# Attention and mixture-of-experts kernel: projection pieces in other quarters of a step, q and k first in a unit

## What is computed

```python
q = (x @ Wq.T + bq).reshape(b, s, 16, 16)             # layer 1; k and v alike
attn = softmax(einsum('bqhd,bkhd->bhqk', q, k) / 4)
x = layernorm(x + (einsum('bhqk,bkhd->bqhd', attn * head_mask, v).reshape(b, s, 256) @ Wo.T + bo))
n = rmsnorm(x, g1)                                    # layer 2
q = q * cos + rotate_half(q) * sin                    # of n @ wq; k alike
h = x + softmax(causal(q @ k.T / 4)) @ v @ wo
logits = rmsnorm(h, g2) @ w_router
y = h + sum over the best 2 experts of weight * (silu(n @ wg) * (n @ wu)) @ wd
x = layernorm(x + y)
```

## Time and profile before

| | us |
|---|---|
| median of 3 runs | 1440.64 (1439.84 to 1443.2) |
| profiled execution | 1439.77 |
| its span, first to last instruction | 1438.0 |
| TensorE busy | 1271.7 (88%) |
| VectorE busy | 956.0 (66%) |
| ScalarE busy | 827.7 (58%) |
| GpSimd busy | 797.1 (55%) |
| mean share of TensorE's clock granted | 0.948 |

### The profile page before, as it was taken

One profiled execution on the slowest core, in us unless ns is written; L12 is line 12 of the kernel. 1 busy time (PEld: TensorE's weight loads), 2 busy tenths in 40 slices (PEclk: granted clock), 3 DMA queues, 4 the chain that ended last, 5 costly groups with the idle time before them and its releaser, 6 DMA issues. The chain is left out here.

```text
span 1438.0 us, 33091 instructions
## 1 busy us (share of the span) xinstructions
PE 1271.7 (88%) x11455; PEld 705.8 (49%) x11456; DVE 956.0 (66%) x1760; ACT 827.7 (58%) x1673; POOL 797.1 (55%) x835
## 2 busy tenths in 40 slices
PE   4999999999989999899999963399999999999990
PEld 1222322223223443344444432378888888888880
DVE  7888888988897888887898613734444444444443
ACT  4178788888878767566667741134434433444334
POOL 5144557547456665856554234056666666666644
PEclk9799999999999999999999975599999999999995
DMA  6345767767687787868675434693322222322326
GB/s 186 69 97 166 174 181 205 202 192 201 180 212 202 224 234 205 228 203 220 175 178 165 120 99 145 182 275 52 46 43 44 47 46 43 47 43 44 44 31 241
DMA packets 159005, 204.46 MB, mean 142 GB/s; under 512 B 31217, under 2 KB 121329, under 8 KB 158897
## 3 DMA queue, kind: packets, MB, share of 16 engines
q1 hardware_dynamic: 141424, 182.55, 46.3%
q0 software_dynamic: 17472, 20.50, 9.1%
HBM read 111.46 MB, written 82.87 MB: 135 GB/s over the span
## 5 line engine op out<-in xcount | busy, mean ns | idle before, releaser
L978 ACT ACTIVATE a_probs<-a_ps_s 128x512 f32<-128x512 f32 (+2 forms) x896 | 459.9, 569 | 156.1 <-PE a_ps_s L746 150.9
L1053 DVE TENSOR_REDUCE a_shift_max<-a_ps_m 128x1 f16<-128x512 f32 x512 | 320.4, 682 | 50.1 <-PE a_ps_m L751 48.8
L751 PE MATMUL a_ps_m<-a_qkx 48*128 48x128 f16 (+3 forms) x1408 | 284.1, 301 | 19.7 <-DVE a_shift_max L1053 9.7
L1650 PE MATMUL e_ps_gu<-e_xT,w_up 128*128 128x256 f16 x2574 | 297.2, 274 | 2.6 <-ACT e_xT L1704 2.6
L746 PE MATMUL a_ps_s<-a_qkx 49*128 49x128 f16 (+3 forms) x1408 | 276.1, 296 | 15.1 <-ACT a_probs L978 15.1
L1650 PEld LDWEIGHTS e_ps_gu<-e_xT,w_up 128*128 x2574 | 249.4, 98 | 35.5 <-issue 6.5
L847 PE MATMUL a_ps_o<-a_probs,a_v_one 128*32 128x512 f32 (+3 forms) x2048 | 234.2, 530 | 2.7 <-ACT a_o L985 2.6
L746 PEld LDWEIGHTS a_ps_s<-a_qkx 49*128 49x128 f16 x1408 | 90.0, 95 | 267.3 <-ACT a_probs L978 155.7
L1586 POOL DMA_INDIRECT h<-e_y,e_put x78 | 125.1, 1604 | 88.8 <-DVE e_y L1746 57.6
L448 POOL TENSOR_TENSOR a_o_half<-a_o_half,a_inv_half 128x512 f32<-128x512 f32 x32 | 40.6, 1269 | 227.3 <-DMA a_inv_half<-a_inv_dram 221.9
L1672 PE MATMUL e_ps_y<-w_down,e_h 128*128 x1326 | 154.1, 273 | 9.3 <-issue 6.7
(11 more groups left out here) (194 smaller groups left out, 1664.4 us busy)
## 6 DMA issues: line engine op xcount, KB each, us to landing
a_qkx<-a_qk_dram SPq DMA_DIRECT2D x192, 128.0 KB, 4.3
a_qk_dram<-a_qk SPq DMA_DIRECT2D x32, 512.0 KB
a_o_dram<-a_o SPq DMA_DIRECT2D x64, 256.0 KB, 2.6
a_o_half<-a_o_dram SPq DMA_DIRECT2D x32, 256.0 KB
a_inv_half<-a_inv_dram SPq DMA_DIRECT2D x32, 256.0 KB
part<-a_part SPq DMA_DIRECT2D x16, 512.0 KB, 5.8
a_q_swap<-a_q SPq DMA_DIRECT2D x64, 128.0 KB
spare<-in_wg SPq DMA_DIRECT2D x16, 352.0 KB, 5.6
```

Of the source, the lines that this page charges most:

```text
L751: return pe.matmul(out, qx[first:first + 48, r, pair, q * P:(q + 1) * P], kx[first:first + 48, r, pair, k0:k1], start=start, stop=stop)
L978: act.activation(dst, src, ACT.Exp).then_inc(exp_out, 1)
L1053: vector.tensor_reduce(out, src, AX.X, ALU.max, negate=True).then_inc(max_out, 1)
L1650: mm = pe.matmul(ps_gu[:, bank, kind, f % 2], w[:, ds(e, 1)].rearrange("p o f -> p (o f)"), xT[:, s, xh, k, :], start=n == 0, stop=n == 5)
```

## The change

The table of pieces is new, and so is where a piece stands. Heavy pieces have table columns 2 and 3 and are done in quarter 2 of their step and quarter 0 of the next; light ones have columns 0 and 1 and come at the end of the quarters 0 and 2, behind the value product. Quarters 1 and 3 have no piece. q and k of unit u + 2 now are the first heavy pieces of a unit, then v, and the output projection comes in g = 3 instead of g = 2. The chain of a causal half is: pieces up to the first quarter of step 2h - 7; swap, `turn_half` and `rope_cos` in the odd step 2h - 7; `rope_sum`, the splits and the store in the even step 2h - 6; the load in 2h - 5; first use in 2h - 3 as before. x of a causal unit is loaded and transposed two steps sooner.

```diff
         kind, v, k = {
-            (0, 0): ("turn", u + 2, 0), (0, 1): ("turn", u + 2, 1), (0, 2): ("v", u + 1, 0), (0, 3): ("v", u + 1, 1),
-            (1, 0): ("parts", u - 3, 1), (1, 1): ("rows", u, 1), (1, 2): ("qk", u + 2, 0), (1, 3): ("qk", u + 2, 1),
-            (2, 0): ("logits", u - 3, 0), (2, 2): ("out", u - 1, 0), (2, 3): ("out", u - 1, 1),
-            (3, 0): ("parts", u - 2, 0), (3, 1): ("rows", u + 1, 0), (3, 2): ("qk", u + 2, 2),
-            (3, 3): ("qk", u + 2, 3)}.get((g, i), (None, 0, 0))
+            (0, 0): ("parts", u - 3, 0), (0, 2): ("qk", u + 2, 0), (0, 3): ("qk", u + 2, 1),
+            (1, 0): ("rows", u, 1), (1, 1): ("parts", u - 3, 1), (1, 2): ("v", u + 1, 1), (1, 3): ("qk", u + 2, 2),
+            (2, 0): ("logits", u - 3, 0), (2, 1): ("turn", u + 3, 0), (2, 2): ("qk", u + 2, 3), (2, 3): ("out", u - 1, 0),
+            (3, 0): ("rows", u + 1, 0), (3, 1): ("turn", u + 3, 1), (3, 2): ("out", u - 1, 1),
+            (3, 3): ("v", u + 2, 0)}.get((g, i), (None, 0, 0))
...
                 if n % 2 == 0:
-                    swap((n + 6) // 2)
-                    load_qk((n + 4) // 2)
                     if g == 0:
                         store_part(u - 3)
                         load_res(u - 1)
-                    elif u + 3 > 0:
-                        load_x(u + 3)
+                        if u + 3 > 0:
+                            load_x(u + 3)
                     store_o(n - 1)
                     for m in weights_at(n - 1):
                         store_weights(m)
                         load_weights(m + 2)
+                    store_qk((n + 6) // 2)
                     load_o(n // 2 - 1)
                 else:
+                    swap((n + 7) // 2)
+                    load_qk((n + 5) // 2)
                     load_rows((n + 1) // 2)
...
-                    store_qk((n + 5) // 2)
...
                 if n % 2 == 0:
-                    h = (n + 6) // 2
-                    if plain(h // 2):
-                        split_high(h)
-                        split_low(h)
                     if g == 0:
                         factors(u - 2)
-                        split_x(u + 2)
                     else:
                         part_low(u - 2)
-                    turn_half(h)
+                    split_high((n + 6) // 2)
+                    split_low((n + 6) // 2)
+                    if g == 2:
+                        split_x(u + 3)
+                    for m in weights_at(n):
+                        split_weights(m)
                 else:
-                    h = (n + 5) // 2
-                    if causal(h // 2):
-                        split_high(h)
-                        split_low(h)
+                    turn_half((n + 7) // 2)
                     if g == 1:
                         bias(u - 1)
+                    for m in weights_at(n):
+                        split_weights(m)
                     normalise((n - 3) // 2)
                     if g == 3:
                         add_residual(u - 1)
-                for m in weights_at(n):
-                    split_weights(m)
...
+            def heavy_piece(n, quarter):
+
+                piece = piece_at(n - 1, 3) if quarter == 0 else piece_at(n, 2) if quarter == 2 else None
...
+            def light_piece(n, quarter):
+
+                piece = None if quarter % 2 else piece_at(n, quarter // 2)
...
-                    a_piece(n, quarter)
+                    heavy_piece(n, quarter)
...
                         weigh(n, quarter - 2)
+                    light_piece(n, quarter)
...
-                    early = (1 if quarter < 2 else 0) if causal(u) else 3
+                    early = 0 if causal(u) and quarter >= 2 else 1
+                    empty_light(n, quarter)
...
-                elif g == 2 and quarter >= 2:
-                    residual(u - 1, quarter - 2)
...
+                if n % G == 3 and quarter % 2 == 0:
+                    residual(n // G - 1, quarter // 2)
...
                     if n % 2 == 0:
                         if quarter < 2:
-                            rope_cos((n + 6) // 2, quarter)
+                            rope_sum((n + 6) // 2, quarter)
                         elif quarter == 3:
                             join_maxima((n + 2) // 2)
                     else:
-                        if quarter < 2:
-                            rope_sum((n + 5) // 2, quarter)
                         if quarter == 1:
                             invert((n - 3) // 2)
+                        if quarter in (1, 2):
+                            rope_cos((n + 7) // 2, quarter - 1)
```

More of the change, by code:

```diff
@@ L110, in attention_layers @@
     for n in range(FIRST, LAST):
-        for i in range(4):
+        for i in (0, 2, 1, 3):
             if piece_at(n, i):
@@ L714, in a_piece @@
                     turn_maxima(u, k)
-                elif kind == "out":
-                    project_out(u, k)
                 elif kind == "parts":
@@ L932, in move_parts, with empty_piece @@
                 act.activation(nT[:, 0].rearrange("p k s -> p (k s)"), ps_x16[:], ACT.Copy).then_inc(piece_out, 1)
-            def empty_piece(n, i):
-                piece = piece_at(n, i)
+            def empty_piece(n, quarter):
+                piece = piece_at(n, 2) if quarter == 2 else piece_at(n - 1, 3) if quarter == 0 else None
                 if piece is None:
@@ L942, in empty_piece, with empty_light @@
                     move_v(u, k)
-                elif kind == "rows":
+            def empty_light(n, quarter):
+                piece = piece_at(n, quarter // 2) if quarter % 2 else None
+                if piece is None:
+                    return
+                kind, u, k = piece
+                if kind == "rows":
                     move_rows(u, k)
@@ L1232, in _ @@
                 for quarter in range(4):
-                    early = causal((n + 3) // G)
+                    empty_light(n, quarter)
                     for i in range(4):
```

113 lines of the change are left out of this document (63 added, 50 removed).

## The result

| | us |
|---|---|
| kernel before, median of 4 runs on the same chip | 1441.9 (1439.8 to 1448.5) |
| changed kernel, median of 4 runs | 1542.4 (1539.5 to 1554.1) |
| ratio | 1.070, 95% interval 1.064 to 1.077 |
| its profiled execution, and span | 1539.5, 1537.7 |

What follows compares the result with a forecast made beforehand. TensorE, busy 88% of the span, was taken as the bound, with VectorE pacing light quarters. Terms -4.5 - 5.2 - 2.4 - 2.5 - 1.5 + 3.5 = -12.6 us took 1439.8 to 1427.2, median 1428; range 1413 to 1443.

Steps and rivals of the forecast that it cites:

- the one on new waits: SP's queue: load_rows waits no longer than before; load_o behind store_qk hardly later, 0, at most +8 us.
- the sign that the text itself named: Sign of being wrong in the profile after: SP waiting in store_qk with load_o behind it; no size given.
- The quarters, plain half: Plain units 1 to 7: alternating heavy and light quarters save 0.6 to 0.7 us a unit, -4.5 us in all.
- the cover: Plain half: light VectorE load in g = 0 hides 1.2 us more from g = 3; +8 bound if gone.
- the walk: One whole plain unit followed quarter by quarter, each instruction starting when engine, input and bank are there; gave 0.65 us gain.
- VectorE in g = 3: Rival, plain half: the cover in g = 0 fails, +13 us, so 1441; chance 0.10.
- Residual and part_low: Causal half: residual two quarters later no longer waits for GpSimd's part_low; -3.7 us of waits, -5.2 with low clock.
- aT: Transposed attention output from GpSimd: two quarters of delay remove TensorE's four waits, -2.4 us, bound 0.
- The rotary chain: Moving rotary work and splits between odd and even steps halves TensorE's 4.9 us waits for maxima, -2.5 us.
- the rival of the ports: Odd steps feeding or running the causal half: GpSimd holds more VectorE products, +24 us, so 1452; chance 0.10.
- The clock: TensorE's half-clock stretch at 790.3 partly goes once stalled maxima go, -1.5 us, bounds -3.4 and +3.4.
- The start: Unit 0: ScalarE's weight copies start 7.2 us later, delaying low parts and row maxima, +3.5 us, bounds 0 and +7.2.

Runs made afterwards that it cites:

- 1500.3: Changed kernel with load_rows moved ahead of swap and load_qk in SP's odd step; 1500.3 us, ratio 1.042.
- 1482.7: Changed kernel with load_rows first in SP's odd step and load_o ahead of store_qk in the even one; 1482.7 us, ratio 1.029.
- 1456.9: Changed kernel with only load_qk moved to the end of SP's odd step, load_o still behind store_qk; 1456.9 us, ratio 1.009.
- the kernel with both edits: Changed kernel with load_qk last in SP's odd step and load_o ahead of store_qk in the even one; 1444.8 us, ratio 1.003.
- the kernel of 1443.1: The kernel with both edits, but load_qk right behind load_inv, ahead of the weights' stores and loads; 1443.1 us, ratio 1.001.
- the two mended ones: The kernel with both edits and the kernel of 1443.1, both with SP's order changed against the changed kernel; 1444.8 and 1443.1 us.

## Why the prediction was wrong

**The step that failed** is the one on new waits: "so load_rows waits no longer than before", which gives the rows no term at all, and for the denominators 0, "hardly later". It asked whether SP's *instruction* would wait for a semaphore. For the rows that was answered rightly: from 480 to 850 SP waits 1.2 us in all in the swap's, the load's and their own line. For the denominators it was not: SP waits 44.1 us in `store_qk` ahead of `load_o` (3.8 before), the sign that the text itself named. It didn't ask at all what was in the queue ahead of the transfer. Moving swap and load from even to odd steps put ten transfers, 1280 KB, ahead of 8 KB that the next step's first score needs; `store_qk` ahead of `load_o` delays the denominators both ways. The price of SP's order is 98 us, of which 85 are the load's line; `load_o` in its old place was worth 18 us in one pair of kernels (1500.3 and 1482.7) and 12 in another (1456.9 and 1444.8), where the text had 0 with 8 as the bound. The text even listed "swap (four DMAs) and load (six) from even to odd steps", and costed only the slack of the load. In the trace of before denominators, rows and inverse go out ahead of the large transfers; that order was there to be read. The bounds fail with it: +8 was the worst case for the denominators, none stood for the rows, and no rival had a queue in it.

The other steps, read where the queue doesn't hide them, in the kernel with both edits or in the changed one:

- *The quarters, plain half (-4.5).* The form was right: quarters of 3.51, 2.52, 3.48, 2.52 us in g = 0 of the changed kernel, and in the steady unit of the kernel with both edits 12.04 + 12.51 + 12.00 + 13.67 = 50.2, where 50.6 - 0.65 = 50.0 was forecast. g = 3 and the next g = 0 give 25.7 (25.8 forecast), g = 1 and g = 2 24.5 (24.2). But this unit is seen in steps 8 to 19 only. In the last plain units, whose g = 3 has the causal maxima and rotary products too, steps 22 and 23 take 13.02 and 14.26 us (12.72 and 12.91 before) and step 27 takes 17.63 (14.13 before): VectorE is full there. So the cover held where the walk was made and failed where it wasn't. In step 27 VectorE is busy 16.95 of 17.7 us, where it had 14.10 of work before. From the end of step 3 to that of step 31, the units 1 to 7 of the term, the kernel with both edits needs 362.0 us and the one before 357.8: +4.2 in place of -4.5. That is the rival "VectorE in g = 3", with another place.
- *Residual and part_low (-3.7 of waits), aT (-2.4).* In the changed kernel both waits are absent from TensorE's list, as forecast, and small ones for the residual's bank come in g = 3 (line 660, 2.7 us in four, in the changed kernel). The time behind them isn't to be seen singly; other waits fill it.
- *The rotary chain (-2.5).* Held products got fewer, from 480 to 850. Of the products on two SBUF inputs that the timeline shows singly, 17 take over 1.4 us before, 8 in the changed kernel (two of them in odd steps) and 9 in the kernel of 1443.1, so the rival of the ports falls. The mean of `rope_cos` fell from 1171 to 866 ns, of `scale_hidden` from 853 to 663, that of `rope_sum` rose from 770 to 935 (before, and the kernel of 1443.1). TensorE's wait for the maxima didn't fall with it: 4.9 us before, 8.0 there and 7.0 in the kernel with both edits (in the changed kernel it is 0.9, beside the 63.8 for the rows). Of the 8.0, 3.5 stand right behind the end of two steps g = 3, and 4.1 in and around three other steps where a product was held. With SP's order mended the term's sign was wrong.
- *The clock (-1.5).* The fall at 790 is away, and others have come, such as the one at 581 above. From 480 to 850 the granted clock is 0.89 in the changed kernel, and 0.98 and 0.99 in the two mended ones, against 0.98 before: with SP's order mended the term is about nothing.
- *The start (+3.5).* Step 0 ends 1.7 us later and step 3 1.9, but that the sign is right is luck. The first row maximum starts at 35.25 us and not 3 to 4 us later than the 35.18 of before. The products of the second to fourth piece took 1.47 us each and not 2.74, so the fourth was moved out at 20.46 and not at 24.52, the copies began at 21.04 and not near 25.1, and VectorE's low parts came no later than before. Where the 1.7 us come from was not found.

Put together: with SP's order mended the change brings no gain: +0.1%, within the noise, and +0.3%, just beyond it. That is nearer to the rival "VectorE in g = 3" (1441) than to the forecast; the gain of the plain half is eaten at the border from plain to causal units.

What stays open: single executions of the last kernels lie between 1427 and 1453 us, and which even step is disturbed differs from kernel to kernel. Why the order of events varies so was not found. The split between SP's time to issue and the transfers' time in the queue (3.6 and 9.1 us at the place shown) was read in one step and not tested by itself. Nor was, for the denominators, the split between SP's wait in `store_qk` and the bytes ahead.

## What to carry to other kernels

When a step of a hand-ordered kernel is moved, write down for every queue what bytes stand ahead of each small transfer in the new order; that the issuing instruction waits for no semaphore says nothing of when its data arrive. Put what the bound engine needs next ahead of what it needs a step later, the largest last. And ask what each instruction ahead waits for: here `load_o` behind `store_qk` and `turn_half` behind `normalise` were late by the waits of others. A walk through a steady unit holds for that unit; the units at the border between two phases carry both loads, and need a walk of their own.

## What the runs showed of the hardware

- A transfer of two times 4 KB took 9.1 us from its issue to its use with 1280 KB issued just ahead of it in the same queue. The 16 KB store behind it took 7.0 us in the median to land, 1.5 in the kernel before, and 1.9 with the large load moved behind it.
- Two small issues from ScalarE take it 1.2 us. TensorE's wait for this transfer fell with them from 63.8 to 0.2 us, and the plain half, where ScalarE is nearly full, took 17 us more.
- A wait of TensorE of 1.8 us was followed by 3 us at half its clock (0.50, so 1.2 GHz); behind 5.3 us of wait the granted clock was 0.58 for 3.5 us. Such a wait cost more than its own length. Not each did: behind one of 1.4 us, at 606.90 in the kernel of 1443.1, the granted clock stayed at 1.00.
- VectorE's product of two SBUF inputs took 1.77 us beside GpSimd's multiplication, 0.63 without it.
